# Other pieces for the first keys and queries, and an earlier projection of the second half

## The reference

```python
    # experts: the second of the two chosen experts sees the input plus half the first one's output
    for i in range(TOP_K):
        eo = _selected_expert(boost, topk_idx[:, :, i], W1, b1, W2, b2)
        outs.append(eo)
        if i < TOP_K - 1:
            boost = boost + ALPHA * jax.lax.stop_gradient(eo)
    fused = sum((topk_vals[:, :, i:i + 1] * outs[i] for i in range(TOP_K)))
    return _layer_norm(residual + fused, ln_gamma, ln_beta)

    # one attention layer
    q = (h @ wq.T + bq_).reshape(bh, sl, H, DH)        # 16 heads of 8 channels
    k = (h @ wk.T + bk_).reshape(bh, sl, H, DH)
    scores = jnp.einsum('blhd,bmhd->bhlm', q, k) * inv_sqrt_d
    w_avg = jax.nn.softmax(scores, axis=-1).mean(axis=1)
    new_w = jax.nn.softmax(CSCALE * w_avg + rel[None], axis=-1)
    sa = jnp.einsum('blm,bme->ble', new_w, h)
    h1 = _ln(h + sa, l1w, l1b)
    h2 = _ln(h1, l2w, l2b)
    ff = jax.nn.relu(h2 @ w1.T + b1_) @ w2.T + b2_
    return (_ln(h2 + ff, l3w, l3b), None)
```

## Time and profile before

| | us |
|---|---|
| median of 3 runs | 2764.98 |
| lowest and highest of them | 2764.63, 2766.47 |
| the profiled execution's own time | 2779.52 |
| span of its trace | 2777.7 |
| busy: DVE, PE, ACT, POOL | 2446.1, 2365.2, 2300.2, 1460.9 |
| PE's first score matmul starts | 530.98 |

### The profile page before, as it was taken

How to read it: one execution, slowest core, us unless ns; L and a number is a source line. 1 busy time by engine, 2 the same in 40 slices (tenths; PEclk the granted TensorE clock), 3 DMA queues, 4 the chain that set the end, 5 groups by cost and what they waited for, 6 DMA issues and landing times.

```text
span 2777.7 us, 93621 instructions
## 1 busy us (share of the span) xinstructions
PE 2365.2 (85%) x38272; PEld 1248.4 (45%) x38289; DVE 2446.1 (88%) x3408; ACT 2300.2 (83%) x4212; POOL 1460.9 (53%) x2897
## 2 busy tenths in 40 slices
PE   5778676489999989999899999999989999999856
PEld 3444365244444544444444444444444444444435
DVE  4987944499999999999999999999999999999956
ACT  5887634389999999999999999999999999999832
POOL 3545554245644566446654466545664456643564
PEclk8998888699999999999999999999999999999978
DMA  4000022202101010110101111011110111100000
GB/s 135 1 1 1 23 79 87 83 25 66 34 36 48 32 58 32 41 48 31 54 29 48 45 34 52 32 48 42 37 48 36 48 38 41 33 35 11 2 1 16
DMA packets 46892, 110.41 MB, mean 40 GB/s; under 512 B 5120, under 2 KB 39808, under 8 KB 42176
## 3 DMA queue, kind: packets, MB, share of 16 engines
q1 hardware_dynamic: 38080, 96.30, 10.1%
q0 software_dynamic: 2432, 5.08, 0.5%
q10 hardware_dynamic: 5952, 3.04, 0.4%
HBM read 79.41 MB, written 29.05 MB: 39 GB/s over the span
## 4 chain that ended last, share of the span: by engine, by line
PE 40%; issue 17%; ACT 13%; DVE 11%; POOL 7%; DMA 2%; DVEq 0%; ACTq 0%; another core or an unknown queue 0%; POOLq 0%; SPq 0%
PE bank L772 12%; PE bank L703 12%; PE bank L783 11%; ACT E L1046 10%; DVE NM L1424 6%; ACT acc L997 1%; POOL H L1672 1%; DMA scratch<-UB 1%; POOL acc L1662 1%; POOL H L1675 1%; PE bank L684 1%; POOL smp L1655 1%; DMA KS<-scratch 1%; PE bank L697 1%; ACT UB L1008 1%
## 5 line engine op out<-in xcount | busy, mean ns | idle before, releaser
L1424 DVE TENSOR_REDUCE NM<-bank 128x1 f32<-128x1024 f32 x1536 | 1798.2, 1206 | 100.0 <-PE bank L772 79.3
L1046 ACT ACTIVATE E<-bank,NM 128x1024 f32<-128x1024 f32 x1536 | 1707.5, 1118 | 185.6 <-DVE NM L1424 159.2
L772 PE MATMUL bank<-KS,QS 72*32 72x512 bf16 x12288 | 960.1, 388 | 183.0 <-ACT E L1046 110.3
L783 PE MATMUL bank<-E,dg 128*32 128x256 f32 x12288 | 927.2, 386 | 1.7 <-ACT acc L997 1.7
L1720 POOL TENSOR_TENSOR dg<-mask,RZ 128x128 f32<-128x128 f32 x384 | 152.9, 398 | 848.2 <-DVE RZ L1434 743.2
L772 PEld LDWEIGHTS bank<-KS,QS 72*32 72x32 bf16 x12288 | 252.5, 96 | 727.3 <-ACT E L1046 585.4
L783 PEld LDWEIGHTS bank<-E,dg 128*32 128x32 f32 x12288 | 384.7, 111 | 293.4 <-issue 63.8
L1046 ACT ACTIVATION_READ_ACCUMULATOR E<-bank,NM 128x1 f32 x1536 | 310.7, 202 | 0.0
L1662 POOL TENSOR_TENSOR acc<-acc,rel 128x256 f32<-128x256 f32 x384 | 272.2, 729 | 7.8 <-ACT acc L997 7.8
L703 PE MATMUL bank<-H,ET 128*32 128x129 f32 x6144 | 189.6, 275 | 6.3 <-DVE ET L1367 6.3
L703 PE MATMUL bank<-hT,WL 128*32 128x256 f32 x2304 | 164.0, 388 | 26.2 <-ACT UB L1008 21.9
(11 more groups left out here) (269 smaller groups left out, 2620.6 us busy)
## 6 DMA issues: line engine op xcount, KB each, us to landing
KS<-scratch SPq DMA_DIRECT2D x24, 1152.0 KB
QS<-scratch SPq DMA_DIRECT2D x72, 384.0 KB
scratch<-UB SPq DMA_DIRECT2D x144, 128.0 KB
WL<-in_wl SPq DMA_DIRECT2D x6, 1091.0 KB, 21.2
first<-in_fill SPq DMA_DIRECT2D x2, 990.0 KB, 7.9
second<-in_fill SPq DMA_DIRECT2D x2, 990.0 KB, 10.0
UNITB<-second ACTq DMA_DIRECT2D x2, 528.0 KB
W<-in_moe_w SPq DMA_DIRECT2D x1, 1032.0 KB
```

Source lines behind the costliest of these rows:

```text
L772: inst = PE_.matmul(bank[x % 3][32 * i:32 * i + 32, k * 512:k * 512 + 512], QS[0:72, half % 2, 4 * hq + i, r0:r0 + 32], KS[0:72, b, k, 4 * ...
L783: inst = PE_.matmul(pb(6)[32 * k:32 * k + 32, 256 * grp:256 * grp + 256], dg[:, x // 4 % 3, x % 4, :], E[:, x % NE, :].rearrange("p (i k c ...
L1046: A_.activation(E[:, x % NE, :], bank[x % 3][:, :], ACT.Exp, bias=NM[:, x % 4:x % 4 + 1], accum_out=ZS[:, quad % 3, j:j + 1]).then_inc(s[" ...
L1424: V.tensor_reduce(NM[:, x % 4:x % 4 + 1], bank[x % 3][:, :], AX.X, ALU.max, negate=True).then_inc(s["rowmax"], 1)
```

## The change

`PROJECT` has the second half's pieces at other steps: `pjq00` and `pjq01` at 189 (were 191), `pjo0` at 190 (192), `pjq10`, `pjq11`, `pjo1`, `part0` and `part1` at 191 (194), `part2` and `part3` at 192 (196).

SP's list for the first sequence's first layer is other. The key load of a half is three loads of 384 KB, one for each of the three copies, with 24 partitions as the outermost dimension on both sides. The query load of half 0 is nine loads of 128 KB with 8 partitions outermost. Half 1's stores are no longer all behind the query loads: two stores (one part of the queries and keys), three query loads, and so on three times. All loads carry the same bytes as before; only the counts that later waits look for are raised to match (`keys_read`, `queries_read`). Later halves keep `stack_k` and `stack_q`.

```diff
@@ PROJECT
 PROJECT = {"PE": {186: ((-4, "pjt"),), 187: ((-4, "pjq00"), (-4, "pjq01")), 188: ((-4, "pjq10"), (-4, "pjq11"), (-3, "pjt")),
-                  191: ((-3, "pjq00"), (-3, "pjq01")), 194: ((-3, "pjq10"), (-3, "pjq11"))},
+                  189: ((-3, "pjq00"), (-3, "pjq01")), 191: ((-3, "pjq10"), (-3, "pjq11"))},
...
@@ new functions
+        def stack_first_k(e, hf):
+            e.wait_ge(s["pq_store"], 96 * (hf + 1))
+            for i in range(3):
+                e.dma_start(KS[24 * i:24 * i + 24, 0, hf, :, :],
+                            scr[0, hf, 1].rearrange("j d h t -> (j d) h t")).then_inc(s[f"stackk0{hf}"], 16)
+
+        def stack_first_q(e, i):
+            e.wait_ge(s["pq_store"], 96)
+            for j in range(3):
+                r0 = i * 24 + j * 8
+                e.dma_start(QS[r0:r0 + 8, 0, :, :], scr[0, 0, 0, i]).then_inc(s["stackq00"], 16)
+
+        def store_part(e, n, j):
+            l, b, hf, u = unit(n)
+            if n < 2:
+                e.wait_ge(s["parts"], 4 * n + (1, 3, 4)[j])
+            else:
+                e.wait_ge(s["split"], before_half(n - 4) + 16)
+            for k in range(2):
+                e.dma_start(scr[b, hf, k, j].rearrange("d h t -> h d t"), PQ[:, 2 * j + k, :]).then_inc(s["pq_store"], 16)
@@ sync
             store_qk(e, 0)
-            stack_k(e, 0)
-            stack_q(e, 0)
-            store_qk(e, 1)
-            stack_k(e, 1)
+            stack_first_k(e, 0)
+            for j in range(3):
+                store_part(e, 1, j)
+                stack_first_q(e, j)
+            stack_first_k(e, 1)
             mixed_of(1)
             fence_sp(e, 1)
             attention_sp(e)
```

More of the change, by code:

```diff
@@ L638, in experts_of, with keys_read, queries_read @@
                                                             skip_runtime_bounds_check_because="the table is held to 7")[1]
+        def keys_read(b, l):
+            return 16 * (l + 1) + (32 if b == 0 else 0)
+        def queries_read(b, hf, l):
+            return 48 * (l + 1) + (96 if b + hf == 0 else 0)
         def fence_pe(e, k):
@@ L763, in scores @@
                 if x % 128 == 0:
-                    e.wait_ge(s[f"stackk{b}0"], 16 * (l + 1))
-                    e.wait_ge(s[f"stackk{b}1"], 16 * (l + 1))
+                    e.wait_ge(s[f"stackk{b}0"], keys_read(b, l))
+                    e.wait_ge(s[f"stackk{b}1"], keys_read(b, l))
                 if x % 64 == 0:
-                    e.wait_ge(s[f"stackq{b}{hf}"], 48 * (l + 1))
+                    e.wait_ge(s[f"stackq{b}{hf}"], queries_read(b, hf, l))
                 if x >= 3:
@@ L1791, in store_qk @@
             if l:
-                e.wait_ge(s[f"stackq{b}{hf}"], 48 * l)
-                e.wait_ge(s[f"stackk{b}{hf}"], 16 * l)
+                e.wait_ge(s[f"stackq{b}{hf}"], queries_read(b, hf, l - 1))
+                e.wait_ge(s[f"stackk{b}{hf}"], keys_read(b, l - 1))
             for j in range(3):
[L1795 to L1800, removed]
+                store_part(e, n, j)
         def rows_of(e, r):
```

## The result

The change takes the median from 2765.12 us (4 runs, 2764.63 to 2766.47) to 2742.15 us (4 runs, 2741.76 to 2746.2). The ratio is 0.9919, with a 95% interval from 0.9903 to 0.9934. That is 23.0 us, where 31.6 were forecast, and 1.15 us outside the range. The last experiments found a version that is faster than both, 2737.92 us beside 2743.93 us for the change and 2765.17 us for before, all three measured together.

The account below looks back on a forecast made before the run. It took PE's 31.02 us wait for late keys, behind slow stores and loads, as the hole to close. 30.4 + 0.4 + 0.8 = 31.6 us off the median 2764.98 gave 2733.4 us, range 2730 to 2741.

Parts of the forecast that it names:

- What bounded the kernel: Before the first scores: PE idle 31.02 us for late keys, from stores landing in 26.18 us and key load in 18.17.
- Do the keys land by then?: SP's load list at the experts' end: keys land between 497 and 499, at worst 501.6, within the floor.
- the floor: Experts' end: POOL's fence at 501.65 lets DVE start its first row maximum at 501.8, 30.4 us earlier.
- The page's rule: New loads: engines up to 16 dividing both outermost dimensions, so 12 and 8; 1.18 MB over 12 takes 3.8 us.
- The steps: Experts' round 3: earlier projection pieces shift its end, taken as 0.4 us earlier, bounds 1.8 earlier to 2.3 later.
- The clock term: Early attention: without the idle stretch PE's clock stays near 1.00, worth 0.8 us, up to 1.9.
- rival 1: First scores: keys land 1 to 6 us after POOL's fence, 2734.5 to 2739.5 us, say 2737; chance 0.13.
- Rival 2: Attention step 3: `f2` waits for its `YS` load in the hole's place, 2737 us if it needs 8; chance 0.04.
- Rival 3: Key and query loads: new form spreads no wider, landing 525.5, 5.5 us better, 2759.5 us; chance 0.03.
- rival 4: SP's queue: 21 transfers pay 2.6 us landing each in series, 54.6 us, nothing gained, 2764 us; chance 0.02.
- rival 5: SP's issue held by a full queue: 4.66 us each, keys 46.4 us late, 2811 us; chance 0.02.

Follow-up runs that it names:

- The last experiments: Third series, on one chip: before 2765.17 us, the change 2743.93, copies written to every third partition 2737.92, that with another load order 2740.8.
- the second profile of before: The kernel before, unchanged, run and profiled again: 2764.16 us, span 2762.2 us.
- The loads alone: The change's loads and stores with the second half's projection at its old steps: 2746.34 us, ratio 0.9941 against before.
- the steps alone: The kernel before with only the change's earlier projection steps, old loads kept: 2765.63 us, ratio 1.0004 against before.
- the interleaved kernel: The change with copy i of row r written to partition 3r+i, not 24i+r: 2756.02 us, ratio 0.9898; run again 2737.92 us, ratio 0.9897.
- the keys first: The change with half 1's stores behind half 0's keys, then half 1's keys, half 0's query loads last: 2766.92 us, ratio 0.994 against before.
- the second series: Runs on a chip of its own, where the kernel before took 2783.6 us.
- the first and third series: Runs on two other chips, where the kernel before took 2764.23 and 2765.17 us.
- the eights: The change with each key load of 24 partitions cut into three of 8: 2776.04 us, ratio 0.998 against before.

## Why the prediction was wrong

**What bounded the kernel: right.** The two long pieces of the earlier trace rows are both an effect of the narrow loads. The length of 55.5 to 55.9 us in four traces with the old loads fell to 31.1 and 29.5, by 24.7 us from the second profile of before, and the medians moved by 23.0. The loads alone did this; the steps alone did nothing.

**The step that failed is "Do the keys land by then?".** It forecast the keys 21.5 to 23.5 us after the first key load (497 to 499 less 475.51), 26.1 by its worse ends. They took 31.1 to the first score. Its terms:

| | forecast | measured |
|---|---|---|
| SP's issues up to the last key loads' wait | 13.7 to 15.1 | 10.2 |
| last store's issue to its landing | 2.1 to 4.5 | 11.6 |
| last key loads' issue to landing (measured: to the first score) | 7 (4.7 to 9.6) | 11.4 |

The store's price came from later halves, where nothing stands ahead of the stores. Here nine of half 0's twelve loads did, five sixths of their bytes; I had seen just that in the kernel before (26.18 us) and took it for gone with the narrow form. The key load's price came from a 384 KB load whose partitions are 128. Both take the queue for empty: the time that the queue needs for what stands ahead was put at nothing, and it is 11.6 us where I had at most 4.5. The sum that was missing is bytes by rate: 3.54 MB of keys and queries and 0.79 MB of stores between 475.5 and the floor, 26 us. That needed 167 GB/s, and the change gave 139. The rate isn't a property of the queue alone: the same 4.33 MB went at 168 GB/s interleaved and at 120 with the keys first.

**The page's rule.** The engine count of the Trainium skill (DMA: Bandwidth & Descriptors, the section on why a DMA increments its semaphore by 16) fits after too: 9.9 of at most 12 were busy. My estimate of 3.8 us from it took the rate per engine of the narrow load, 26 GB/s, and it fell to 13.0; 11.4 us were measured, landing included.

**The floor** was right as a mechanism (POOL's fence, which the interleaved kernel in the second series started on) and too late in its place: 26.1 us after the first key load in the first profile (501.65 - 475.51), 23.1 and 22.9 in the other two of before, 24.2 in after. This took 2 to 3 us from the margin, and made no cost alone.

**The steps.** I gave them 0.4 us of gain within 1.8 earlier and 2.3 later. In the first and third series round 3 is 0.2 to 0.7 us longer with them, inside the bounds and with the other sign, and they bring the keys nothing. The parts do come earlier, part 3 ends 13.1 us after the rows' issue (468.32 - 455.18) and not 17.3 (484.84 - 467.53). I had worked out 11.7 (479.2 - 467.53), 1.5 too early. But the stores that carry them then stood in the queue.

**The clock term** (0.8 us) has no support. The granted clock was to stay near 1.00 from 500 to 550. In after PE waited 9.59 us, and it was 0.52 from 500 to 515, 0.83 from 515 to 525 and 0.90 from 525 to 560. PE's clock falls in the first scores even without a long wait. The interleaved kernel of the second series started its first score at 509.39, 0.17 us behind the fence, and then had 2.11 us of idle time for ACT. Its stretches (length, busy by engine, granted clock, DMA share, GB/s):

```profile
500.00:509.00 9.00, 5.44 (x41) 4.62 (x41) 2.51 (x11) 2.91 (x11) 4.81 (x6) 1.00 0.65 181
509.00:512.00 3.00, 1.67 (x26) 0.74 (x26) 1.62 (x2) 0.28 (x1) 1.04 (x2) 0.85 0.07 22
512.00:525.00 13.00, 10.06 (x80) 1.85 (x80) 12.65 (x25) 10.13 (x19) 1.44 (x2) 0.50 0.48 133
```

The level is 2.4 GHz until the fence and 1.2 GHz from 512 to 525. What the lower level costs there wasn't measured.

**The rivals.** What happened is rival 1, at 0.13: the keys land after POOL's fence, by 8.0 us at DVE and not the 1 to 6 that I allowed. Rival 2 didn't occur: `f2` came 9.58 us after DVE's start as before. But SP could issue its `YS` load only 7.0 us after POOL's end (486.87 to 493.84), not 1.3: it waited for the last scatters to land, with the key loads under way. Rival 3 is refuted by the 9.9 busy engines, rival 4 by the 31.1 us that the 21 transfers took and not 54.6, and rival 5 for this kernel by SP's 0.38 us for an issue; in the eights SP did need 1.97 us for each of three loads. With rival 1 given its right size the forecast would have been 33.7 us (518.71 to 485.0, by the second profile) less 8, 25.7 off, near the 23.0 measured. That the forecast missed by 8.6 us and not by more is luck in part: the first profile showed DVE's idle time 3.3 us too short (30.4, not 33.7).

## What to carry to other kernels

Before transfers are called hidden, add up all bytes that share their queue between the first issue and the floor, and divide by a rate measured for that form; landing times of lone transfers didn't add up to it here. Don't count on the rate of one engine being kept when more take part (here it halved), and look at which partitions one transfer writes. An idle stretch ends at the later of two chains, so give both as distances from a common event and take them from more than one profiled execution. Moving a producer earlier brought nothing here, as its store stood behind other loads in the same queue.

## What the runs showed of the hardware

- Rate for each busy DMA engine with rows of 16 KB: 26.7 GB/s with 3 engines busy; 13.0 with 9.9 busy and 24 neighbouring partitions for each load; 17.1 with 8.6 busy and every third partition. The 26.7 held beside POOL's scatters, and nearly without them the form of 24 neighbouring partitions gave 14.3, with 11.1 busy.
- A store of 128 KB landed 11.6 us after its issue behind nine loads of the new form, 26 us behind four of the old form, and 5.6 us behind nine interleaved loads.
- The same key bytes in loads of 8 neighbouring partitions went with a keys' length of 47.6 us and not 31.1 (on another chip).
- SP's time to issue a load: 0.34 to 0.40 us for one to 24 or 8 neighbouring partitions, 0.64 to 0.81 us (once 0.97) with every third partition, 0.73 to 0.88 us with a copy of 3 outermost. Behind much queued work it was more: 1.97 us for each of three loads of 8 partitions in the eights, 4.66 us for each of three with a copy of 3.
- The experts' end shifted by 17 us between two executions of the same kernel (484.88 and 501.65), and the median of before by 19 us between series on different chips.
